# Attention 0 of a four-layer decoder: row lengths from half-width statistics, both inversions ahead of all scalings, the scales spread over six PSUM banks

## The reference, cut to what matters

```python
def _l2norm(x, eps=EPS_NORM):
    n = jnp.linalg.norm(x, axis=-1, keepdims=True)
    return x / jnp.maximum(n, eps)
...
q = qn @ q_w.T + q_b
k = kn @ k_w.T + k_b
v = vn @ v_w.T + v_b
q = _l2norm(q)
k = _l2norm(k)
...
beta = jnp.clip(jax.nn.softplus(beta_param), BETA_MIN, BETA_MAX)
scores = jnp.einsum('bhqd,bhkd->bhqk', q, k)
scores = scores * (beta / math.sqrt(DH))[None, :, None, None]
...
attn = jax.nn.softmax(scores, axis=-1)
out = jnp.einsum('bhqk,bhkd->bhqd', attn, v)
```

## Time and profile before

| | us |
|---|---|
| median of three executions | 2401.74 |
| the three | 2400.6, 2401.74, 2408.82 |
| the profiled execution, its own time | 2409.55 |
| its span, from the first to the last instruction | 2407.7 |
| attention 0 in the span | 26.3 to about 155 |

### The profile page before, as it was taken

One profiled execution on the slowest core, in us unless ns is written; L12 is line 12 of the kernel. 1 busy time (PEld: TensorE's weight loads), 2 busy tenths in 40 slices (PEclk: granted clock), 3 DMA queues, 4 the chain that ended last, 5 costly groups with the idle time before them and its releaser, 6 DMA issues. The chain is left out here.

```text
span 2407.7 us, 36395 instructions
## 1 busy us (share of the span) xinstructions
PE 1841.4 (76%) x11991; PEld 1118.9 (46%) x11991; DVE 1733.5 (72%) x5481; ACT 1102.8 (46%) x3070; POOL 751.8 (31%) x657
## 2 busy tenths in 40 slices
PE   6988899962888999999888875665565555556888
PEld 2545446542455777754465553333233333233453
DVE  5346442368775666667646579999999999997665
ACT  3663432251315777721323654555555555555411
POOL 1200045015434555400034403444333333332230
PEclk8999999965999999999998996666566565667979
DMA  5000100310000000000200000000000000000000
GB/s 221 2 1 1 46 11 29 108 65 1 2 2 1 2 1 1 2 1 0 99 2 1 1 1 1 1 1 1 1 1 1 1 1 1 1 1 1 1 1 18
DMA packets 10597, 37.89 MB, mean 16 GB/s; under 512 B 1344, under 2 KB 7488, under 8 KB 9136
## 3 DMA queue, kind: packets, MB, share of 16 engines
q1 hardware_dynamic: 8880, 33.05, 3.6%
q0 software_dynamic: 1536, 2.59, 0.4%
HBM read 30.17 MB, written 5.51 MB: 15 GB/s over the span
## 5 line engine op out<-in xcount | busy, mean ns | idle before, releaser
L4052 PE MATMUL psum<-work 32*128 32x256 f32 x512 | 130.9, 656 | 291.6 <-ACT work L4170 291.6
L4232 DVE MATCH_REPLACE8 work<-work 128x256 f32<-128x256 f32 x768 | 306.0, 412 | 0.0
L4295 POOL TENSOR_TENSOR work<-work 128x1024 f32<-128x1024 f32 x63 | 148.3, 2354 | 484.0 <-ACT work L4170 460.7
L4229 DVE MAX8 work<-work 128x8 f32<-128x256 f32 x768 | 267.2, 412 | 0.0
L4052 PEld LDWEIGHTS psum<-work 32*128 32x128 f32 x512 | 77.9, 312 | 318.3 <-ACT work L4170 162.7
L1357 POOL TENSOR_TENSOR work<-work 128x256 f32<-128x256 f32 (+1 forms) x128 | 103.1, 826 | 127.4 <-DVE work L1306 123.6
L4170 ACT ACTIVATE work<-work 128x256 f32<-128x256 f32 x256 | 128.4, 502 | 0.0
L4077 PE MATMUL psum<-work,tiles 128*8 128x256 f32 x512 | 116.3, 606 | 8.2 <-ACT work L4180 7.4
L4297 POOL TENSOR_TENSOR work<-work 128x1024 f32<-128x1024 f32 x63 | 119.2, 1892 | 6.1 <-DVE work L4254 1.2
L4168 ACT ACTIVATE work<-psum,work 128x256 f32<-128x256 f32 x256 | 117.4, 459 | 0.0
L1254 ACT ACTIVATE work<-work 128x128 f32<-128x128 f32 (+1 forms) x256 | 112.8, 451 | 0.0
(11 more groups left out here) (645 smaller groups left out, 4681.6 us busy)
## 6 DMA issues: line engine op xcount, KB each, us to landing
big_weights<-L0f_dram SPq DMA_DIRECT2D x1, 6103.5 KB, 28.1
big_weights<-L_dram SPq DMA_DIRECT2D x1, 5772.0 KB, 16.4
big_weights<-L_dram SPq DMA_DIRECT2D x1, 4952.5 KB, 16.9
choice_rows<-tiles SPq DMA_DIRECT2D x2, 1024.0 KB, 10.5
tiles<-choice_rows SPq DMA_DIRECT2D x8, 256.0 KB, 4.7
big_weights<-L_dram SPq DMA_DIRECT2D x1, 2027.0 KB, 21.4
big_weights<-L_dram SPq DMA_DIRECT2D x1, 1644.5 KB, 14.1
big_weights<-L0f_dram SPq DMA_DIRECT2D x1, 1644.5 KB, 6.2
```

The lines of the kernel that those rows point to most:

```text
L4052: mm = nc.tensor.matmul(scores(n)[:, u, :], qb[head, tile % 2, u % 2 * P:(u % 2 + 1) * P], kb[head, tile % 2, :], start=True, stop=True, t ...
L4229: ch.step(v.max(top8[:, n % 2, u, r, :], src[:, u, :]))
L4232: ins = v.match_replace(raw[:, n % 2, u, :], top8[:, n % 2, u, r, :], src[:, u, :], REPLACED)
L4295: ch.link(g.tensor_tensor(mine, mine, rest[:, n % 2], ALU.subtract))
```

## The change

The sums of squares of four parts are now made together, in two passes of 256 columns: the first four matmuls take the left halves of the four parts into the upper 16 rows of the four bands, the next four add the right halves in the lower 16 rows. The statistics of a half of the parts are then 128x256 and no longer 128x512. Part 7 is projected between `lengths(0)` and `lengths(1)`. ACT squares all eight parts and takes both roots behind them; a root of a constant is added behind the logarithm, so that the root's table is fetched there. DVE clamps and inverts both halves and then scales all eight parts. PE spreads each part with two matmuls of 256 columns, into six banks (6, 7, 0, 1, 2, 3, 6, 7), so that only parts 6 and 7 wait for a scaling, that of parts 0 and 1. The scores of step 0 wait for six scalings, because they use banks 0 to 3. The wait for `aux_p` moves from the body's start to the first addition to the residual, in step 7. `c.unread` is issued at three other places: two matmuls ahead of the projections, three ahead of the spreads, four ahead of the scores; the four between the scalings go.

```diff
-    root = c.work[:, 4 * 2 * 2 * S:4 * 2 * 2 * S + 2 * CH].rearrange("p (s x) -> p s x", x=CH)
-    inv = a.take(2, CH)
+    HF = CH // 2
+    root = c.work[:, 4 * 2 * 2 * S:4 * 2 * 2 * S + 2 * HF].rearrange("p (s x) -> p s x", x=HF)
+    inv = a.take(2, HF)
...
+    spread_bank = [6, 7, 0, 1, 2, 3, 6, 7]
...
-            def lengths(n):
-                i, s = n // 2, n % 2
-                pe.wait_ge(c.squared.sem, c.squared.at(n + 1))
-                mm = nc.tensor.matmul(c.psum[band[n % 4], 4 + n // 4, :], ones[:, 0:32], square[:, s, ch[i]], start=True,
-                                      stop=True, tile_position=(0, 32 * (n % 4)))
-                if n % 4 == 3:
-                    mm.then_inc(c.lengths_ready.sem, 1)
-
-            for n in range(2 * NC):
-                i, s = n // 2, n % 2
+            c.unread(5, 2)
+
+            def project_rows(n):
                 if n >= 4:
                     pe.wait_ge(c.rows_copied.sem, c.rows_copied.at(n - 3))
-                nc.tensor.matmul(c.psum[:, n % 4, :], (wq, wk)[s], n2[:, ch[i]], start=True, stop=True) \
+                nc.tensor.matmul(c.psum[:, n % 4, :], (wq, wk)[n % 2], n2[:, ch[n // 2]], start=True, stop=True) \
                     .then_inc(c.rows_ready.sem, 1)
-                if n >= 3:
-                    lengths(n - 3)
-            for n in range(2 * NC - 3, 2 * NC):
-                lengths(n)
-            for n in range(2 * NC):
-                if n >= 2:
-                    pe.wait_ge(c.rows_normed.sem, c.rows_normed.at(n - 1))
-                if n == 4:
-                    c.unread(6, 4)
+
+            def lengths(h):
+                pe.wait_ge(c.squared.sem, c.squared.at(4 * h + 4))
+                for half in range(2):
+                    for n in range(4 * h, 4 * h + 4):
+                        lo = n // 2 * CH + half * HF
+                        mm = nc.tensor.matmul(c.psum[band[n % 4], 4 + h, 0:HF], average_of[:, half, :],
+                                              square[:, n % 2, lo:lo + HF], start=(half == 0), stop=(half == 1),
+                                              tile_position=(0, 32 * (n % 4)))
+                mm.then_inc(c.lengths_ready.sem, 1)
+
+            def spread(n):
                 if n % 4 == 0:
                     pe.wait_ge(c.inverted.sem, c.inverted.at(n // 4 + 1))
-                nc.tensor.matmul(c.psum[:, 6 + n % 2, :], avg[band[n % 4], :], inv[band[n % 4], n // 4, :], start=True,
-                                 stop=True, tile_position=(32 * (n % 4), 0)).then_inc(c.spread.sem, 1)
+                if n >= 6:
+                    pe.wait_ge(c.rows_normed.sem, c.rows_normed.at(n - 5))
+                for half in range(2):
+                    mm = nc.tensor.matmul(c.psum[:, spread_bank[n], half * HF:(half + 1) * HF], value_of[band[n % 4], half, :],
+                                          inv[band[n % 4], n // 4, :], start=True, stop=True,
+                                          tile_position=(32 * (n % 4), 0))
+                mm.then_inc(c.spread.sem, 1)
+
+            for n in range(2 * NC - 1):
+                project_rows(n)
+            lengths(0)
+            project_rows(2 * NC - 1)
+            lengths(1)
+            c.unread(6, 3)
+            for n in range(2 * NC):
+                spread(n)
+            c.unread(4, 4)
...
-                    pe.wait_ge(c.rows_normed.sem, c.rows_normed.at(2 * i + 2))
+                    pe.wait_ge(c.rows_normed.sem, c.rows_normed.at(max(2 * i + 2, 6)))
...
+            nc.scalar.activation(warm, c.w("one"), ACT.Sqrt)
             for n in range(2 * NC):
                 i, s = n // 2, n % 2
                 act.wait_ge(c.rows_copied.sem, c.rows_copied.at(n + 1))
                 nc.scalar.activation(square[:, s, ch[i]], rows[s][:, ch[i]], ACT.Square).then_inc(c.squared.sem, 1)
-                if n in (5, 7):
-                    h = n // 7
-                    act.wait_ge(c.lengths_ready.sem, c.lengths_ready.at(h + 1))
-                    nc.scalar.activation(root[:, h, :], c.psum[:, 4 + h, :], ACT.Sqrt).then_inc(c.rooted.sem, 1)
+            for h in range(2):
+                act.wait_ge(c.lengths_ready.sem, c.lengths_ready.at(h + 1))
+                nc.scalar.activation(root[:, h, :], c.psum[:, 4 + h, 0:HF], ACT.Sqrt, scale=float(P)).then_inc(c.rooted.sem, 1)
...
                 v.reciprocal(inv[:, h, :], root[:, h, :]).then_inc(c.inverted.sem, 1)
-                for n in range(4 * h, 4 * h + 4):
-                    i, s = n // 2, n % 2
-                    dve.wait_ge(c.spread.sem, c.spread.at(n + 1))
-                    v.scalar_tensor_tensor(rows[s][:, ch[i]], rows[s][:, ch[i]], beta if s == 0 else float(P // G),
-                                           c.psum[:, 6 + n % 2, :], ALU.mult, ALU.mult).then_inc(c.rows_normed.sem, 1)
-            dve.wait_ge(c.aux_p.sem, c.aux_p.at(1))
+            for n in range(2 * NC):
+                i, s = n // 2, n % 2
+                dve.wait_ge(c.spread.sem, c.spread.at(n + 1))
+                v.scalar_tensor_tensor(rows[s][:, ch[i]], rows[s][:, ch[i]], beta if s == 0 else float(2 * P // G),
+                                       c.psum[:, spread_bank[n], :], ALU.mult, ALU.mult).then_inc(c.rows_normed.sem, 1)
...
                     dve.wait_ge(c.out_product.sem, c.out_product.at(b))
+                    if b == 1:
+                        dve.wait_ge(c.aux_p.sem, c.aux_p.at(1))
```

More of the change, by code:

```diff
@@ L1440, in layer0_attention @@
     soft = a.take(6)
-    beta = a.take(1)
+    beta, warm = a.take(1), a.take(1)
     biases, rows = (bias_q, bias_k), (q, k)
     head_rows = c.w("L0a_head_rows")
-    ident, ones, avg = c.w("identity"), c.w("ones"), c.w("average")
+    ident, average_of, value_of = c.w("identity"), c.w("average_of"), c.w("value_of")
+    spread_bank = [6, 7, 0, 1, 2, 3, 6, 7]
     wq, wk, wv, wo, bo = (c.w("L0a_" + s) for s in ("wq", "wk", "wv", "wo", "bo"))
@@ L1622, in _ @@
             chain.link(v.tensor_scalar(soft[:, 5:6], soft[:, 4:5], 0.1, 10.0, ALU.max, ALU.min))
-            chain.step(v.tensor_scalar(beta, soft[:, 5:6], float(P // G / np.sqrt(8.0)), None, ALU.mult))
+            chain.step(v.tensor_scalar(beta, soft[:, 5:6], float(2 * P // G / np.sqrt(8.0)), None, ALU.mult))
             for n in range(2 * NC):
```

## The result

| | us |
|---|---|
| before, median of five | 2400.6 (2399.38 to 2408.82) |
| changed, median of five | 2387.81 (2386.76 to 2388.24) |
| ratio changed to before | 0.9938, 95% interval 0.9927 to 0.995 |
| the changed kernel's profiled execution | 2387.04, span 2385.2 |
| changed kernel once more, in a later session, ten executions | 2392.87 (2386.37 to 2398.39) |

The change makes the kernel faster: by 12.8 us (0.62%) in the first comparison and by 8.9 us (0.41%) in the second. The forecast was 2388.6 and 13.1 us. The fastest executions of the two kernels lie 12.6 and 13.0 us apart in the two comparisons (2399.38 and 2386.76; 2399.35 and 2386.37).

What follows compares the result with a forecast made beforehand. A chain of waits in attention 0's head, no engine full. Inversions 3.5, projections 2.5, spreads and scalings some 4, the rest clock, make 13.1 us: 2401.7 - 13.1 = 2388.6, own range 2385 to 2391, widened to 2384 to 2396.

Steps and rivals of the forecast that it cites:

- What bounds: Head of attention 0: no engine full, a chain of waits; what it ends earlier, the body and later stages start earlier.
- Projections, 2.5 earlier: Head: part 7's projection starts at 39.8 against 42.31, without alternation with sums; two unread matmuls charged 0.9 us.
- Roots and inversions: Head: inversions of 256 columns take 1.74 each; with clamps the two cost 4.0 us instead of 7.5.
- Spreads and scalings in one run: Head: spreads hidden behind the second inversion, eight scalings without waits from 46.95 to 52.1; some 4 us gained.
- Scores and the clock: Head's end: first exponential at 52.2 against 63.51, third step's at 56.7 against 69.84, at full clock; 13.1 us gained.
- Costed at nothing: Root's table load moved to the front, and the wait for `aux_p`, with POOL done at 60, needed about 69.
- The rule that speaks against it: Sums and spreads: more, shorter matmuls at some 60 cycles each could add 0.8 us, leaving a gain of 12.3.
- Rival A: New head: the clock falls, at about 48; gain 7.5 +- 1, time 2394; chance 0.17.
- Rival B: Before's timed executions lack the profile's half clock in the head, worth 3.5 to 3.8 us; 2392; chance 0.25.
- C: Body: the clock stays low, each step's hop costs 0.96 us more; kernel 17 slower, 2418; chance 0.03.
- D: Head: spreads or sums don't overlap and hold DVE, giving back 2 us; 2390.6; chance 0.07.

Runs made afterwards that it cites:

- The wide kernel: The changed kernel with sums, roots, clamps, inversions and spreads again 512 columns wide, all orders kept; 2399.03 us, ratio to before 0.9974.
- scalings between: The changed kernel with DVE's old order: clamp, invert, four scalings, and again for the second half; 2393.47 us, ratio to before 0.9949.
- old wait: The changed kernel with the wait for POOL's addition to the residual back ahead of the body; 2395.96 us, ratio to before 0.9969.
- the three kernels made from before: Before with projections 0 to 6 ahead of the sums (2398.23 us), and before with more unread matmuls in two different amounts (2400.78 and 2394.68 us).
- the projections first: Before with projections 0 to 6, sums 0 to 3, projection 7, sums 4 to 7, all 512 columns wide; 2398.23 us, ratio to before 0.9978.
- the first try of more unread matmuls: Before with four unread matmuls ahead of the first spreads and ten in place of four ahead of the fifth; 2400.78 us, ratio 0.9987.
- the version with earlier scores: The changed kernel without unread matmuls ahead of projections and scores, other spread banks, no clamps, exponential's table loaded behind the roots; 2386.46 us, ratio to before 0.9935.

## Why the prediction was right

**What bounds.** A chain of waits in the head, with the body and all behind it starting as much earlier: right. The body from the third exponential to the last output projection took 83.52 us in both profiles (123.75 - 40.23 and 110.54 - 27.02, counted from the first matmul).

**Projections, 2.5 earlier.** Measured 2.6 from the first matmul, the two unread ones included. They cost 0.8 of the 0.9 charged. Only 1.7 of the 2.6 reached the first inversion, since the first clamp stood right behind the last part's copy before (2.28 from that part's projection to the first inversion), and now the last square and the first root stand between (3.21), as the sum had it.

**Roots and inversions.** First inversion forecast at 43.15, or 13.5 behind the first matmul; measured 13.28. 1.74 each, measured 1.75. The second one's end was forecast 17.3 behind, and measured 16.97. The wide kernel shows the 3.5.

**Spreads and scalings in one run.** Eight scalings in 5.1; measured 5.0 (46.78 to 51.79), with no gap. The overlap of the four bands' matmuls was also right: 1.07 for one `lengths` where 1.05 was taken.

**Scores and the clock.** Forecast of the third exponential 27.1 behind the first matmul; measured 27.02. That they agree within 0.1 is in part luck: the second inversion ended 0.3 ahead of the forecast, and the two steps behind the first exponential took 2.34 and 2.33 where 2.25 was taken. The split of the gain was less good than its sum: of the 13.2, 3.5 are width; 1.7 the earlier first inversion (14.98 to 13.28), unread matmuls included; 4.4 the clock, where about 3 was taken; the remaining 3.6, by subtraction, the order and the banks, for which the sum had some 4. These parts are not independent: the width, the order, the banks and POOL's wait, each undone alone, also brought the low clock back, and so cost more than their share.

**Costed at nothing.** The table load for the root stands at 30.00 in the changed kernel and the first square at 34.50, so it is off the path, as forecast; no run moves it alone. POOL's addition ended at 59.51, forecast 60, and with the wait at its new place DVE waits for POOL nowhere from the first matmul of the stage to the end of the body.

**The rule that speaks against it.** By the Trainium skill, TensorEngine Tiling (Array Packing), Instruction Overhead, the added matmuls were to cost up to 0.8, by the prediction's estimate. The traces show the eight half-width sums in 1.07 us and four of full width, in the kernel with wide statistics, in 1.06 and 1.07; the first half's spreads took 1.17 with eight matmuls and 1.14 with four. No such addition is to be seen.

**Rival A**, a low clock in the new head, did not come in either profile; the longest idle time was 1.50, where 1.6 was forecast. But five of the experiments on the changed kernel show how near it was: the clock fell behind or in PE idle times of 2.53, 4.78 and 5.47 us (wide statistics, scalings between, old wait), and behind 1.25 and 1.32 where the spreads had two banks or the unread matmuls were gone. **Rival B** was half right. It was right that the profile of before stood above its median for a reason that does not belong to the change, but wrong in the place: its later stages took 2254.3 us, and those of the three kernels made from before 2242.8 to 2244.9. In the profiles of the two kernels that keep before's spreads and banks, with the projections first and with the first try of more unread matmuls, the low clock was there as well, so it is not an accident of one execution. That the executions that were only timed have it too is likely and not shown. **C** and **D** did not come. That 13.1 and 12.8 agree so closely is luck in part: a second session gave 8.9.

**What a measurement can tell.** The prediction took 0.5%, 12.0 us, as the least that can be told, and gave "same" a chance of 0.45 on that ground. The 95% intervals measured reach some 0.12% and 0.14% to either side, so that even the 8.9 us of the second session are clear of no change.

## What to carry to other kernels

A short chain through several engines is costed well by distances between starts in one trace, one hop at a time; here a sum of some fifteen hops was off by 0.1 us at its end and by up to 0.3 on the way. Ask of each edit whether it leaves PE idle ahead of a chain of short products, since such a gap (2.5 to 5.5 us in three experiments here) was paid twice, by itself and by the half clock behind it. Unread matmuls paid for themselves where they filled such a gap and ended before the wait did (4.4 us), hardly where they ran on past it (1.3), and not at all ahead of the projections (0.8 lost). Compare the changed stage in the traces when the rest of a long program scatters by more than the gain, and look at what a faster stage will run into on an idle engine's side, as the wait for POOL, before the gain is counted.

## What the runs showed of the hardware

The granted clock fell shortly behind, or in, an idle time of PE, and then stayed at 0.50 while PE was busy. The falls in the head came up to 1.0 us behind the end of PE's last idle time, which lasted from 0.83 (kernel before) to 4.78 us; with the old wait for POOL the fall lay inside the 5.47. In the kernel without unread matmuls PE was then busy 94% of the ten us at 0.50; with two banks 13.00 of 13.00 (the profile models where a matmul ends). What filled these stretches were spreads, whose operands lie on 32 partitions, scores, and unread matmuls, whose operands lie on 128. The Trainium skill, TensorE: Matmul & The Clock Gate, Part 1, says that an idle time brings the clock down and a busy one brings it back; the trace agrees for the projections at the front (clock 0.50 up to 33.67 before and 33.96 in the changed kernel, and 1.00 behind); for the stretches of spreads and scores it does not agree so plainly, as there PE was busy almost throughout and the clock stayed at 0.50 for 10.2 us (no unread matmuls), 13.7 (two banks) and 17.1 (before). Over the thirteen profiles the clock rose 3.7 to 4.8 us behind the first matmul of the stage.

A table load of ACT took 1.28 us and nothing more: in the changed kernel one ran from 28.39, and the next instruction of ACT started at 29.68. The one ahead of the exponential ran from 50.04 and cost nothing, as the scores came later; in the version with earlier scores the masked copies end at 50.71 (48.14 + 2.57) and the exponential starts at 51.27, between which it would not have fitted.

The largest surprise is the scatter of unchanged code: the same instructions from the last output projection of attention 0 to the end took 2242.8 to 2254.3 us in the thirteen profiles. In two of the three later sessions the slower executions of a kernel had the lower mean granted clock (changed kernel: 2386.37 at 0.840, 2398.39 at 0.832; before: 2399.99 at 0.837, 2411.03 at 0.828). In the remaining one this held for some kernels and not for others (wide statistics: 2396.51 at 0.840, 2399.03 at 0.843), so the clock does not account for all of the scatter, and what moves it is not shown.
